# Attention on TensorE in column tiles of 32, with the loops over pairs of heads written out

## What is computed

```python
# block 0: attention with relative positions (12 heads of 16 channels), then an MLP
attn = einsum('bqc,bkc->bqk', q * scale, k)
attn = attn + rel_h[:, :, :, :, None] + rel_w[:, :, :, None, :]     # per head, 2304 x 2304
attn = softmax(attn, axis=-1)
out  = einsum('bqk,bkc->bqc', attn, v)
x    = shortcut + (out @ proj_w + proj_b)
x    = x + (gelu(layernorm(x) @ mlp_w1 + mlp_b1) @ mlp_w2 + mlp_b2)
# block 1: layernorm, 2-D real FFT, a two-layer block-diagonal filter, softshrink, inverse FFT,
# residual, then layernorm and a second MLP with GELU
```

## Time and profile before

| | us |
|---|---|
| three runs | 1268.88, 1270.88, 1267.50; median 1268.88 |
| profiled execution, its own time | 1272.69 |
| its span in the trace | 1270.9 |
| TensorE matmul busy | 1115.2 (88%) |
| VectorE busy | 874.0 (69%) |
| ScalarE busy | 700.9 (55%) |
| TensorE clock granted, mean of the span | 0.919 |

### The profile page before, as it was taken

How to read it: one execution, slowest core, us unless ns; L and a number is a source line. 1 busy time by engine, 2 the same in 40 slices (tenths; PEclk the granted TensorE clock), 3 DMA queues, 4 the chain that set the end, 5 groups by cost and what they waited for, 6 DMA issues and landing times.

```text
span 1270.9 us, 23592 instructions
## 1 busy us (share of the span) xinstructions
PE 1115.2 (88%) x7694; PEld 548.8 (43%) x7694; DVE 874.0 (69%) x1702; ACT 700.9 (55%) x1008; POOL 190.4 (15%) x159
## 2 busy tenths in 40 slices
PE   3955789999999799979997999999988786693997
PEld 2544123333333233323332333333447674482676
DVE  3746768888888588868885888888526764132442
ACT  3645056766666466646674666766774432131444
POOL 2620045000000000000000000000035662000443
PEclk9975589999999899989998999999999877696999
DMA  7697788565564374635564364736300010121111
GB/s 109 155 251 227 179 163 129 80 98 89 87 100 76 59 118 66 109 59 89 87 94 83 50 108 74 114 56 99 63 17 21 19 29 10 45 59 43 30 38 29
DMA packets 83298, 108.40 MB, mean 85 GB/s; under 512 B 14349, under 2 KB 75569, under 8 KB 82996
## 3 DMA queue, kind: packets, MB, share of 16 engines
q1 hardware_dynamic: 82660, 105.17, 43.9%
q10 hardware_dynamic: 528, 1.77, 1.1%
HBM read 85.47 MB, written 21.44 MB: 84 GB/s over the span
## 4 chain that ended last, share of the span: by engine, by line
PE 73%; DMA 7%; DVE 7%; issue 6%; ACT 3%; POOL 3%; SPq 1%; ACTq 0%; POOLq 0%; DVEq 0%
PE ps L1021 52%; PE ps L1173 20%; DVE mx_p L1465 2%; DVE xh L111 2%; POOL hid L748 1%; DVE stage_lo L1437 1%; DMA m_d<-mneg 1%; DMA mask<-in_c_mask 1%; ACT hid L943 1%; DMA rel_d<-stage_lo 1%; ACT hid_f L949 1%; POOL rstd L119 1%; PE ps L1027 1%; DMA q_w<-qw_d 1%; DMA kq_d<-khl 1%
## 5 line engine op out<-in xcount | busy, mean ns | idle before, releaser
L1465 DVE TENSOR_REDUCE mx_p<-ps 128x1 f32<-128x464 f32 (+1 forms) x1080 | 620.9, 630 | 110.6 <-PE ps L1021 79.2
L896 ACT ACTIVATE prob<-ps 128x768 f32<-128x768 f32 x648 | 492.2, 808 | 294.1 <-PE ps L1021 292.3
L1021 PE MATMUL ps<-kc,qc 112*128 112x464 f16 (+1 forms) x1080 | 401.5, 373 | 25.6 <-DVE mx_p L1465 13.8
L1021 PE MATMUL ps<-qv,ka 113*128 113x384 f16 x1296 | 355.4, 330 | 18.8 <-issue 9.0
L1173 PE MATMUL ps<-prob,v_ext 128*32 128x384 f32 x2592 | 280.2, 504 | 0.5 <-ACT prob L896 0.5
L1021 PEld LDWEIGHTS ps<-kc,qc 112*128 112x128 f16 x1080 | 105.4, 98 | 250.4 <-DVE mx_p L1465 163.9
L1021 PEld LDWEIGHTS ps<-qv,ka 113*128 113x128 f16 x1296 | 123.7, 101 | 117.8 <-issue 33.0
L1173 PEld LDWEIGHTS ps<-prob,v_ext 128*32 128x32 f32 x2592 | 51.3, 108 | 116.0 <-issue 91.5
L721 POOL COPY v_ext<-v_all 128x288 f32 (+1 forms) x12 | 5.1, 427 | 607.7 <-PE ps L1173 607.7
L1021 PE MATMUL ps<-w_dn,hid 128*96 128x192 f16 x864 | 84.1, 262 | 7.7 <-ACT hid L943 7.7
L1021 PEld LDWEIGHTS ps<-w_dn,hid 128*96 128x96 f16 x864 | 81.4, 134 | 13.9 <-ACT hid L943 8.8
(11 more groups left out here) (104 smaller groups left out, 866.3 us busy)
## 6 DMA issues: line engine op xcount, KB each, us to landing
qv<-rel_d SPq DMA_DIRECT2D x216, 144.0 KB
qv<-kq_d SPq DMA_DIRECT2D x108, 216.0 KB
qc<-rel_d SPq DMA_DIRECT2D x24, 216.0 KB, 4.0
xin<-in_x SPq DMA_DIRECT2D x12, 288.0 KB, 3.6
kq_d<-khl SPq DMA_DIRECT2D x24, 144.0 KB, 2.4
q_h<-kq_d SPq DMA_DIRECT2D x9, 288.0 KB, 4.9
q_w<-qw_d SPq DMA_DIRECT2D x9, 288.0 KB, 7.0
rel_d<-stage_hi SPq DMA_DIRECT2D x4, 648.0 KB, 8.2
```

Source lines behind the costliest of these rows:

```text
L896: nc.scalar.activation(prob[:, s4(p, s), :].rearrange("p (a b) -> p a b", a=2), ps[:, 3 + 2 * (s % 2):5 + 2 * (s % 2), 0:CW], ACT.Exp).the ...
L1021: return nc.tensor.matmul(o, l, r, start=start, stop=stop)
L1465: nc.vector.tensor_reduce(mx_p[:, q * GT + k // MP, k % MP:k % MP + 1], ps[:, slot, 0:min(MW, N - k % MP * MW)], AX, ALU.max).then_inc(uni ...
```

## The change

1. `scores` and the "max" units: each matmul with 128 weight columns becomes four with 32 weight columns, at `tile_position=(0, c)`, c = 0, 32, 64, 96 (`mm_quarters`). All four read the same moving columns and write the same bank, on 32 partitions each. The semaphore is raised by the last of the four.
2. "mt": the f32 transpose becomes an ordinary matmul with the identity, at `tile_position=(0, 0)`.
3. "out": each of the four matmuls with 96 weight columns becomes three with 32.
4. The loops over pairs of heads on TensorE, ScalarE, VectorE, SyncE and GpSimd become Python loops: the same periods in the same order, with constants in place of registers.

The values matmuls, the order of the units, the buffers and all waits are as before.

```diff
-def rounds(eng, count, body):
-    body(0)
-    with eng.Fori(1, count) as c:
-        body(c)
...
-            rounds(sp, NH // 2 - 1, two_periods)
+            for i in range(NH // 2 - 1):
+                two_periods(i)
...
-            with pool.Fori(1, NH // 2) as i:
+            for i in range(1, NH // 2):
...
-            with act.Fori(1, NH // 2 - 1) as i:
+            for i in range(1, NH // 2 - 1):
...
+            def mm_quarters(bank, w, l, r):
+                for c in range(0, 128, 32):
+                    ins = nc.tensor.matmul(ps[c:c + 32, bank, 0:w], l[:, c:c + 32], r, start=True, stop=True,
+                                           tile_position=(0, c))
+                return ins
...
-                    mm(ps[:, slot, 0:end - w], qc[0:HD + 2 * S, hp, qt * 128:(qt + 1) * 128],
-                       kc[0:HD + 2 * S, hp, w:end]).then_inc(unit_ps, 1)
+                    mm_quarters(slot, end - w, qc[0:HD + 2 * S, hp, qt * 128:(qt + 1) * 128],
+                                kc[0:HD + 2 * S, hp, w:end]).then_inc(unit_ps, 1)
...
-                    nc.tensor.transpose(ps[0:GT, slot, 0:128], mx[:, q * GT:(q + 1) * GT], ident[:, :])\
-                      .then_inc(unit_ps, 1)
+                    nc.tensor.matmul(ps[0:GT, slot, 0:128], mx[:, q * GT:(q + 1) * GT], ident[:, :],
+                                     start=True, stop=True, tile_position=(0, 0)).then_inc(unit_ps, 1)
...
-                        ins = mm(ps[0:T, slot, t * 2 * (HD + 1):(t + 1) * 2 * (HD + 1)],
-                                 o_sb[:, (NQ * p + group) % 2, t * T:(t + 1) * T],
-                                 sel[:, :, :].rearrange("p h c -> p (h c)"))
+                        for c in range(0, T, 32):
+                            ins = nc.tensor.matmul(ps[c:c + 32, slot, t * 2 * (HD + 1):(t + 1) * 2 * (HD + 1)],
+                                                   o_sb[:, (NQ * p + group) % 2, t * T + c:t * T + c + 32],
+                                                   sel[:, :, :].rearrange("p h c -> p (h c)"), start=True,
+                                                   stop=True, tile_position=(0, c))
...
-                ins = mm(ps[:, 3 + 2 * (s % 2) + j, 0:CW], ka[0:QR + 1, p, k0:k0 + 128],
-                         qv[0:QR + 1, (p + q) % 2, v, j * CW:(j + 1) * CW])
+                ins = mm_quarters(3 + 2 * (s % 2) + j, CW, ka[0:QR + 1, p, k0:k0 + 128],
+                                  qv[0:QR + 1, (p + q) % 2, v, j * CW:(j + 1) * CW])
...
-            with pe.Fori(1, NH // 2 - 1) as i:
-                half[0] = i
+            for i in range(1, NH // 2 - 1):
...
-            with dve.Fori(1, NH // 2 - 1) as i:
+            for i in range(1, NH // 2 - 1):
```

More of the change, by code:

```diff
@@ L1098, in ring_unit @@
                 if kind == "max" and q == 0 and k == 0:
-                    pe.wait_ge(c_in[hp], 64 * (heads_like(n, p) + 1 + (p if other else 0)))
+                    pe.wait_ge(c_in[hp], 64 * ((n // 2) + 1 + (p if other else 0)))
                 if not (isinstance(count, int) and count < RING):
@@ L1138, in norm_transposed @@
                 transposes(xh2[0], bank).then_inc(done, 1)
-            def heads_like(n, p):
-                return half[0] if half[0] is not None else n // 2
-            half = [None]
             for u, unit in enumerate(before):
@@ L1157, in scores @@
                 if s % GS == 0 and j == 0:
-                    pe.wait_ge(qv_in[(p + q) % 2], 160 * (3 * heads_like(n, p) + (3 * p + q) // 2 + 1))
-                ins = mm(ps[:, 3 + 2 * (s % 2) + j, 0:CW], ka[0:QR + 1, p, k0:k0 + 128],
-                         qv[0:QR + 1, (p + q) % 2, v, j * CW:(j + 1) * CW])
+                    pe.wait_ge(qv_in[(p + q) % 2], 160 * (3 * (n // 2) + (3 * p + q) // 2 + 1))
+                ins = mm_quarters(3 + 2 * (s % 2) + j, CW, ka[0:QR + 1, p, k0:k0 + 128],
+                                  qv[0:QR + 1, (p + q) % 2, v, j * CW:(j + 1) * CW])
                 if j == 1:
@@ L1180, in period @@
                 at, u = units_of(n), 0
-                pe.wait_ge(k_in[p], 48 * (heads_like(n, p) + 1))
+                pe.wait_ge(k_in[p], 48 * ((n // 2) + 1))
                 def slot_units(x):
@@ L1217, in _ @@
             period(1, 1)
-            with pe.Fori(1, NH // 2 - 1) as i:
-                half[0] = i
+            for i in range(1, NH // 2 - 1):
                 period(2 * i, 0)
                 period(2 * i + 1, 1)
-            half[0] = None
             wait_consts(pe)
```

## The result

| | before | after |
|---|---|---|
| median of the runs, us | 1268.49 | 1220.89 |
| lowest to highest | 1267.50 to 1270.88 | 1218.11 to 1223.77 |
| profiled execution, its own time | 1272.69 | 1223.77 |

The account below looks back on a forecast made before the run. TensorE sets the pace, VectorE close behind. Shorter groups (58.5 us), the last group (1) and the jumps (32.3) take 92 us off the profiled 1272.7, giving 1181, or 1177 as median; range 1158 to 1230.

Parts of the forecast that it names:

- The change of shape: TensorE, each values block: going into the tiled shape and out again costs 0.23 us, which goes in full.
- Four tiles for the price of one matmul: TensorE scores and maxima: four 32-column matmuls take as long as one of 128 columns, 0.163 us a score, addition 0.
- Rival A: TensorE: each four costs 24 ns more than one plain matmul, weights or stagger exposed; 1227 us, chance 0.16.
- Rival C: TensorE: no weight load of a next four is hidden, 9 us a group; near 1490 us, chance 0.05.
- Rival B: TensorE's instruction supply becomes the bound: 62 ns a load and matmul, 21.8 us a group; 1281 us, chance 0.07.
- "mt" and "out": TensorE, each group: "mt" stays at 0.11 us, "out" goes from 0.70 to 0.44 us.
- VectorE as the next bound: VectorE, busy 18.1 us a group, coupled with TensorE's 18.3, holds the group at 18.9 us.
- The jumps: Three jumps back in the loops over pairs of heads cost 10.8 us each; writing loops out saves 32.3 us.
- The price of the instructions: TensorE's straight code: about 700 instructions a group, a block in some 6.2 us, arriving in time; costed at nothing.
- rival D: Written-out loops bring nothing net: dense straight code stalls on instruction blocks by 32 us; 1209 us, chance 0.10.

Follow-up runs that it names:

- the last kernel: Against the kernel with paced qv loads: qc and kc loads go between qv loads, ka loads and MLP weights moved later; 1154.8 us, ratio 0.909.
- the faster kernel: Changed kernel with SyncE issuing the nine loads of the next qv one by one over the running group's steps, not in one burst; 1162.2 us, ratio 0.915.

## Why the prediction was right in direction and half off in size

- **The change of shape, 0.23 us a block**: right; the maxima made plain give 0.22.
- **Four tiles for the price of one matmul**: right. Two scores are 0.33 us apart before and after, the values 0.65 a block as summed. Rival A (24 ns on each four) falls, although the measured time, 1221, lies nearest to its 1227: a total can't tell which case holds, but an undisturbed group of 18.15 us against A's 20.3 does. Rival C falls too, and with it, for this kernel, the rule of the Trainium skill, "TensorE: Matmul & The Clock Gate", Part 3, The mechanism, that a load overlaps only with matmuls of another row group: fours on the same rows, 0.165 us apart, leave no room for a load that isn't hidden. Rival B falls: 349 pairs in 18.15 us are 52 ns each, below the 62 ns of the earlier trace rows. (The trace has 1094 matmul records in a head, some 50 ns each: "out" shows as 24 matmul records a group where 12 were counted.)
- **"mt" and "out"**: the sum of 18.3 for a group met 18.15; the large terms came out as forecast, so the two together are off by some 0.15 at most. "Out" was put at 0.44; its matmuls begin at 444.95 us in the last kernel and the score behind them at 445.27, 0.32 later.
- **VectorE as the next bound, 18.9 us a group**: wrong, mis-sized by 0.75 x 35 = 26 us, in the kernel's favour. The step that failed is to read VectorE's busy share (18.1 us a group) as its floor. The same reductions were recorded as 54.39 us a head before and as 52.64 in the faster kernel. Their recorded lengths, 0.63 us, reach into one another when they follow closely, since the shortest distance between two starts in the trace is 0.53 to 0.55.
- **The jumps, 32.3 us**: right in the traces (31.5); 27 us in the medians.
- **The price of the instructions, "nothing"**: wrong, and this is where the gain went. The forecast named it as rival D, but at 32 us and with a chance of 0.10. It cost 1220.9 - 1154.8 = 66 us, 58.7 of them for the qv loads alone; its mechanism, a stall on blocks in dense code, was right, and its size half of what came. The step that failed is "if a block asked for in advance comes as quickly, it is in time": it took the latency of one fetch and not what stands before it. The right question was what the DMA engines have in hand when a block is asked for. Nine loads, 1.5 MB in all and issued at once, keep them full for 8.5 to 11.5 us in every group, and the prediction itself gave a block 6.2 us. Both numbers could be had before the change; they weren't put beside one another. In the kernel before, a block lasted some 16 us (884 loads and matmuls in a head of 61.7 us, 230 to a block; 13 was written in an expectation above), and the burst was covered.

The Trainium skill's page "Runtime: NRT & Kernel Launch", section Instruction fetch mechanics, has the instructions come in blocks that the sequencer asks for itself, at a cost that is mostly hidden, while a taken branch breaks the sequence. On the jumps the traces agree (10.8 us each). On "mostly hidden" they agree where a block lasts 16 us; at 6 us, behind a burst of nine loads, it isn't. That a block came in time through 9 us of full engines with the loads one by one, and late with three or nine at once, speaks for a wait behind what is already queued. How a block gets its turn on a DMA engine stays open: no run here separates the number of queued loads from the time that they take.

The sum made again: 92 forecast, plus 26 from VectorE, less 66 for the stalls, is 52. Measured: 47.6 in the medians, 48.9 in the profiled executions.

## What to carry to other kernels

Where matmuls in column tiles and plain ones alternate, look for a gap on either side of each tiled block; the same work in one shape throughout costs the array nothing extra, but four times the instructions. Before an engine's instruction rate is raised, set the time in which it uses up a block of them beside the stretches in which bursts of loads fill the DMA engines, and break these loads up by waits on the work's own progress; the mark of the trouble is a stop, put down to "issue", ahead of an instruction that waits for nothing. A busy share near one doesn't make an engine the bound: halve its work and look.

## What was not expected of the hardware

- TensorE stops for 1 to 3.7 us in most groups where a block of its instructions falls behind a burst of nine loads, and the lower clock behind a stop of 3 us adds to it (0.58 granted over the 3.5 us that follow). With the same loads one by one the engines are still full for 9 us once in a head (share 1.06 from 427 to 436 us), and TensorE doesn't stop there.
- A jump back into the denser code costs more: 14 us a round with the tiles, 10.8 without.
- The four column tiles run independently: one matmul of a four began at 454.31 us, the other three 3.15 us later. Behind "mt", which takes tile (0, 0) alone, one tile stays some 0.2 us behind the others in the last kernel: of the next four scores three begin at 451.24 us and one at 451.45, which is after three of the four that follow (451.41). So the last matmul of a four, which raises the semaphore, isn't there the last to end; whether a reader can come too early by that wasn't tried.
- VectorE's busy time for the same reductions fell from 54.4 to 52.6 us a head when they followed one another more closely.
